# A fused two-layer adapter block on one core: Wb and the first two tiles of W1 multiplied by pairs of k, and five smaller reorderings

## The chip, the core and the metric

The kernel runs on one core of a Trainium2 chip. Such a core has TensorE (PE, with PEld for its weight loads), VectorE (DVE), ScalarE (ACT), GpSimd (POOL) and SyncE (SP, which here only issues transfers), each with an instruction stream of its own, and 16 DMA engines. The streams meet only at semaphores. The metric is device time in microseconds (us), less is better.

## The reference, cut to what matters

Two layers, each a conditional projection followed by a routed low-rank (LoRA) stage, for x of 2048 tokens by 1024 features:

```python
x = x + L0_ffn(L0_cond(x))          # top-2 gated adapters, then top-1 gated low-rank stage
x = x + L1_ffn(L1_cond(x))

# L1_cond: per batch b an adapter slot
out = einsum('bti,oi->bto', x, W) + b + lora_out * SCALING   # A, B of slot adapter_mapping[b]
# L1_ffn: top-2 of 8 experts of rank 16
base = xf @ W_base.T + b_base
logits = xf @ W_router.T
lora = einsum('td,erd->ter', xf, A) ... * SCALING
```

`W` of L1_cond is called W1 below, and `W_router`, `A` and `W_base` of L1_ffn side by side are called Wb: 8 + 128 + 1024 = 1160 columns.

## The kernel before, in words

**What is precomputed.** Nothing lies between L1_cond and L1_ffn but linear maps, so the kernel first multiplies them into one matrix, M = W1 x Wb (plus the identity for the residual), and the main part, one slot for each of the 8 batches, then multiplies x by M. This text is about the part that makes M and about what stands between, the first 166 us or so.

**How M is made.** W1 is cut into eight tiles s = 0 to 7 of 128 rows (rows in the order of `M_ROWS`). Wb lies in SBUF in eight slices k of 128 rows, and by columns in three chunks c = 0, 1, 2 of 240, 460 and 460 (`CHUNKS`). Each product is done as three matmuls of fp32r (`three`, L1332 to L1336): each operand is split into a part hi, which ACT copies, and a part lo, which DVE computes as raw minus hi (`lo`, L850). So a part that lands from DRAM goes DMA, ACT, DVE, PE, in that order. `m_chunk(par, c)` is 8 slices of k times three, 24 matmuls, into a PSUM bank of tile par = s mod 2.

**The opening.** Both tiles of W1 and all of Wb are split as they land. `WF_PARTS` (L274) cuts the tiles of W1, `F_PARTS` (L282) cuts Wb; SP issues the loads in the order of L346 to L355, ACT and DVE split in the same order (L670, L1144), PE takes chunk 0 of both tiles first, then chunk 1 of both by pairs of k, then chunk 2 of tile 0 and of tile 1 (L1377 to L1397). The four engines go by hand-written order alone.

**After it, by the same matmul stream.** (1) The gathered adapters of the slots (`bs_raw`, eight transfers whose addresses SP reads from `ids`) are multiplied by Wb, L1399 to L1407; `keep_fe` stores the result to DRAM (`fe_hi_dram`, `fe_lo_dram`, L377). (2) R0 x B0 (`d0w`), then R0 x W0 for eight tiles of W0, whose homes in SBUF (`W0_HOME`) are used again and again: tile 1 lies where the first tile of W1 was, tile 4 where B0 was. (3) Tiles s = 2 to 7 of W1, and between them the first slot's small products.

**`fold_rows(s)`** (L1120) finishes tile s: `add_ident` on DVE adds the identity in PSUM, ACT splits tile s + 2 of W1 (`w1_split`) into the place that tile s leaves, ACT copies the finished columns, DVE computes their lo parts (`Mdir`, `G`). Before it uses PSUM bank par again, PE waits for `m_lo`, and for `w1_lo` before it uses the split tile (L1447, L1465).

**`b_times(k)`** (L1091) accumulates b x Wb in `b_acc` on DVE: for hi and lo of slice k and the three chunks one instruction each, six in all. There are 8 such k. PE reads `b_acc` in `bias_part` only after tile 7's chunk 0 (L1470).

Of the kernel before, what the change touches and what calls it, by code (L numbers as in the profile page):

```python
# [24 lines left out]
def adaln_ffn(nc, xT, lang_ids, slot_ids, W0, R0, A0, B0, Bw, W1, b1, lora_As, lora_Bs, F0, F1, F2, b_base, B1, out):  # L25
# [11 lines left out]
    with ctx:  # L37
# [122 lines left out]
        wf_in, wf_hi, wf_lo = [sem(f"wf_in{i}") for i in range(5)], sem("wf_hi"), sem("wf_lo")  # L160
# [113 lines left out]
        WF_PARTS = [(0, 0, 2), (0, 2, 4), (1, 0, 4), (0, 4, 8), (1, 4, 8)]  # L274
# [7 lines left out]
        F_PARTS = [(0, 0, 2), (0, 2, 4), (0, 4, K), *((c, k, k + 2) for c in (1, 2) for k in range(0, K, 2))]  # L282
# [45 lines left out]
        def _(sp):  # L328
# [54 lines left out]
            sp.wait_ge(fe_stored, 32)  # L383
# [45 lines left out]
            sp.wait_ge(fe_stored, 64)  # L429
# [63 lines left out]
        def _(gp):  # L493
# [63 lines left out]
        def _(act):  # L557
# [132 lines left out]
            hi_half(bs_in, 16 * NB, k_first(bs_hi_t), by_batch(bs_raw), bs_hi)  # L690
# [38 lines left out]
            for s in range(2, LAST):  # L729
# [49 lines left out]
            act.wait_ge(fe_stored, 64)  # L779
# [69 lines left out]
        def _(dve):  # L849
# [481 lines left out]
        def _(pe):  # L1331
# [373 lines left out]
```

## Time and profile before

| what | value |
|---|---|
| median of 3 runs | 466.93 us (466.07 to 467.23) |
| the profiled execution | 465.49 us, span of its instructions 463.6 us |
| PE busy | 446.5 us, 96% of the span |
| DVE, ACT, POOL busy | 307.6, 154.8, 68.6 us |
| read from DRAM, written | 27.07 MB, 9.59 MB |

The profile is one execution. Its busy times say which engine carries the span; its waits and its timeline say when that engine stood still and for whom. A matmul's end is modelled and overlaps the next one's start, so the distance of two starts is what one costs.

### The profile page before, as it was taken

Reading aid. Unit: us, or ns where it says so; the run is one execution under the profiler, and the core shown is the slowest. Engines: PE = TensorE matmul, PEld = TensorE weight load, DVE = VectorE, ACT = ScalarE, POOL = GpSimd, SP = SyncE. Lnnn points to the kernel's source line nnn. Section 1 sums busy time; section 2 is a strip of 40 time slices with the busy share of each in tenths; the row PEclk is TensorE's granted clock in tenths of the full one; section 3 lists DMA queues with packets and bytes.
Section 4 is the critical chain, followed back from the end, with each engine's and each line's share of the span. In section 5 each row is a group of like instructions: output and inputs, shape, how many; then the busy total and the mean of one; then the engine's idle time right before and its main releaser. Section 6 shows DMA issues by size and latency. Waiting matters only on the chain.

```text
span 463.6 us, 7831 instructions
## 1 busy us (share of the span) xinstructions
PE 446.5 (96%) x2758; PEld 414.8 (89%) x2758; DVE 307.6 (66%) x916; ACT 154.8 (33%) x325; POOL 68.6 (15%) x61
## 2 busy tenths in 40 slices
PE   4999989999969999999999999999999999999997
PEld 4988989999968898889899999999999999999986
DVE  4856675656996788578467648738747755864852
ACT  5754363202122463234233224224323423321310
POOL 1100000000002411402402222120140230220110
PEclk9999999999998999999999999999999999999999
DMA  8973651101110101104102201211210310300202
GB/s 270 386 216 134 207 216 45 47 0 47 53 39 6 50 23 49 47 17 145 47 11 104 79 17 62 98 46 62 98 45 17 139 54 1 111 7 1 107 2 90
DMA packets 16287, 37.08 MB, mean 80 GB/s; under 512 B 2551, under 2 KB 7929, under 8 KB 16254
## 3 DMA queue, kind: packets, MB, share of 16 engines
q1 hardware_dynamic: 16158, 36.66, 23.1%
q8 instruction: 18, 0.29, 0.3%
q14 instruction: 15, 0.12, 0.1%
q0 software_dynamic: 96, 0.00, 0.0%
HBM read 27.07 MB, written 9.59 MB: 79 GB/s over the span
## 4 chain that ended last, share of the span: by engine, by line
PE 72%; DVE 14%; SPq 6%; DMA 3%; issue 2%; ACT 2%; DVEq 0%; ACTq 0%
PE banks L1334 22%; PE banks L1336 22%; PE banks L1335 22%; SPq L330 5%; DVE b_acc L1097 3%; DVE G L852 3%; PE banks L1422 2%; PE banks L1567 2%; DMA ws_lo_raw<-in_W_dram 2%; DMA b0lo_raw<-in_W_dram 1%; DVE ws_lo L852 1%; PE banks L1349 1%; SPq L362 1%; DVE x_raw L998 1%; DVE left L852 1%
## 5 line engine op out<-in xcount | busy, mean ns | idle before, releaser
L1334 PE MATMUL banks<-G,left 128*128 128x460 f32 x224 | 88.0, 393 | 0.0
L1335 PE MATMUL banks<-G,left 128*128 128x460 f32 x224 | 82.9, 370 | 0.0
L1336 PE MATMUL banks<-G,left 128*128 128x460 f32 x224 | 82.9, 370 | 0.0
L1334 PE MATMUL banks<-WbThi,ws_hi 128*128 128x460 f32 (+1 forms) x192 | 68.4, 356 | 9.8 <-DVE WbTlo L852 5.5
L509 POOL TENSOR_TENSOR xTlo<-x_raw,xThi 128x512 fp32r<-128x512 f32 x28 | 37.9, 1373 | 209.7 <-DVE hg L910 107.4
L1336 PE MATMUL banks<-WbThi,ws_lo 128*128 128x460 f32 (+1 forms) x192 | 67.0, 349 | 0.0
L1335 PE MATMUL banks<-WbTlo,ws_hi 128*128 128x460 f32 (+1 forms) x192 | 66.9, 348 | 0.0
L561 ACT ACTIVATE left<-x_raw 128x512 fp32r<-128x512 f32 x64 | 38.7, 627 | 59.9 <-DVE x_raw L998 29.3
L1334 PEld LDWEIGHTS banks<-WbThi,ws_hi 128*128 128x128 f32 x192 | 38.0, 198 | 13.1 <-issue 6.2
L1334 PEld LDWEIGHTS banks<-G,left 128*128 128x128 f32 x224 | 42.5, 190 | 4.5 <-DVE wzTlo L852 0.3
L1336 PEld LDWEIGHTS banks<-G,left 128*128 128x128 f32 x224 | 42.0, 188 | 4.7
L1335 PEld LDWEIGHTS banks<-G,left 128*128 128x128 f32 x224 | 42.3, 189 | 2.6
L998 DVE TENSOR_TENSOR x_raw<-banks,x_raw 128x512 f32<-128x512 f32 x32 | 22.0, 690 | 30.5 <-PE banks L1336 29.6
L1335 PEld LDWEIGHTS banks<-WbTlo,ws_hi 128*128 128x128 f32 x192 | 38.1, 198 | 2.9
L1336 PEld LDWEIGHTS banks<-WbThi,ws_lo 128*128 128x128 f32 x192 | 38.0, 198 | 2.7
L1029 DVE TENSOR_TENSOR ybuf<-banks,ybuf 128x460 f32<-128x460 f32 x48 | 29.6, 629 | 11.4 <-PE banks L1336 10.5
L1334 PE MATMUL banks<-Mdir,left 128*128 128x256 f32 x128 | 36.5, 285 | 0.2 <-DVE left L852 0.2
L1335 PE MATMUL banks<-Mdir,left 128*128 128x256 f32 x128 | 35.9, 281 | 0.0
L1336 PE MATMUL banks<-Mdir,left 128*128 128x256 f32 x128 | 35.9, 281 | 0.0
L509 POOL TENSOR_TENSOR left<-x_raw,left 128x512 fp32r<-128x512 f32 x16 | 20.7, 1311 | 99.4 <-DVE hg L910 74.5
L852 DVE SCALAR_TENSOR_TENSOR left<-x_raw,left 128x512 fp32r<-128x512 f32 x48 | 32.2, 685 | 2.8 <-ACT left L561 1.9
L1336 PE MATMUL banks<-C0hi,xTlo 128*128 128x272 f32 x112 | 32.3, 288 | 0.0
(208 smaller groups left out, 964.1 us busy)
## 6 DMA issues: line engine op xcount, KB each, us to landing
x_raw<-in_xT_dram SPq DMA_DIRECT2D x16, 512.0 KB, 3.7
out_dram<-ybuf SPq DMA_DIRECT2D x14, 512.0 KB, 2.7
WbTlo_raw<-in_F_dram SPq DMA_DIRECT2D x8, 460.0 KB, 8.3
x_raw<-in_W_dram SPq DMA_DIRECT2D x6, 512.0 KB, 3.7
ws_lo_raw<-in_W_dram SPq DMA_DIRECT2D x3, 512.0 KB, 5.1
w0s_lo_raw<-in_W_dram SPq DMA_DIRECT2D x2, 512.0 KB, 9.5
Fbuf<-fe_hi_dram SPq DMA_DIRECT2D x16, 64.0 KB
ws_lo_raw<-in_W_dram SPq DMA_DIRECT2D x3, 256.0 KB, 5.0
```

Source lines behind the costliest of these rows:

```text
L330: return sp.dma_start(dst, src).then_inc(s, 16)
L509: return gp.tensor_tensor(out_, a, b, ALU.subtract)
L561: act.activation(dst, src, ACT.Copy).then_inc(ready, 1)
L852: return dve.scalar_tensor_tensor(out=out_, in0=src, scalar=scale, in1=hi.bitcast(F32), op0=ALU.mult, op1=ALU.subtract)
L998: dve.tensor_tensor(raw_quarter(raw, g), by_half(bank), raw_quarter(raw, g), ALU.add).then_inc(x1_sum, 1)
L1029: return dve.tensor_tensor(ybuf[tile][:, y0:y0 + n], bank, base, ALU.add).then_inc(ready, 1)
L1097: dve.scalar_tensor_tensor(out=b_acc[:, c0:c0 + w], in0=Wb_of[c][n][:, k, :].bitcast(F32), scalar=bcol[:, k:k + 1], in1=b_acc[:, c0:c0 + w ...
L1334: pe.matmul(out_, l[0], r[0], start=start, stop=False, **kw)
L1335: pe.matmul(out_, l[0], r[1], start=False, stop=False, **kw)
L1336: return pe.matmul(out_, l[1], r[0], start=False, stop=stop, **kw)
L1422: ins = pe.matmul(banks[:, C0_BANKS[k // 2] + k % 2, 0:2 * RC], w, R0T[:, j, :], start=j == 0 and n == 0, stop=j == K - 1 and n == 1)
L1567: pe.matmul(y, hsT[half][:, :], Fbuf[:, s], start=False, stop=True, skip_group_check=True)\
```

## The change

It has six parts. (a) The opening: the two tiles of W1 and Wb land and are split by pairs of k over all columns, and PE multiplies both tiles by each part as it comes (`first_two`). W1's two tiles now land in six parts, Wb still in eleven. (b) `b_times` takes a range of halves (hi or lo of one k) in place of a k, and the 16 halves are dealt out to other places of DVE's stream. (c) GpSimd issues the two `ids` loads at once. (d) The split of `bs_raw` stands before `fold_rows(0)` on ACT and DVE. (e) The product of the adapters is stored chunk by chunk, six stores in place of two, and W0's tile 3 is loaded between them. (f) In `fold_rows` on ACT, `w1_split` no longer waits for the identity's addition.

```diff
-        WF_PARTS = [(0, 0, 2), (0, 2, 4), (1, 0, 4), (0, 4, 8), (1, 4, 8)]
+        WF_PARTS = [(0, 0, 2), (1, 0, 2), (0, 2, 4), (1, 2, 4), (0, 4, K), (1, 4, K)]
-        F_PARTS = [(0, 0, 2), (0, 2, 4), (0, 4, K), *((c, k, k + 2) for c in (1, 2) for k in range(0, K, 2))]
+        F_PARTS = [(0, 0, 2), (1, 0, 2), (2, 0, 2), (0, 2, 4), (1, 2, 4), (2, 2, 4),
+                   (0, 4, K), (1, 4, 6), (2, 4, 6), (1, 6, K), (2, 6, K)]
...
+            def store_fe(c):
+                s = slice(CHUNKS[c][0], CHUNKS[c][0] + CHUNKS[c][1])
+                sp.wait_ge(fe_hi, c + 1)
+                sp.wait_ge(fe_lo, c + 1)
+                sp.dma_start(fe_hi_dram[0:P, s], fe_keep[0][:, s].bitcast(F32)).then_inc(fe_stored, 16)
+                sp.dma_start(fe_lo_dram[0:P, s], fe_keep[1][:, s].bitcast(F32)).then_inc(fe_stored, 16)
+
+            store_fe(0)
+            store_fe(1)
             sp.wait_ge(fe_done, 3)
             load_w0(3)
-            sp.wait_ge(fe_hi, 3)
-            sp.wait_ge(fe_lo, 3)
-            sp.dma_start(fe_hi_dram[0:P, :], fe_keep[0][:, :].bitcast(F32)).then_inc(fe_stored, 16)
-            sp.dma_start(fe_lo_dram[0:P, :], fe_keep[1][:, :].bitcast(F32)).then_inc(fe_stored, 16)
+            store_fe(2)
             sp.wait_ge(d0w_done, 1)
             load_w0(4)
             sp.wait_ge(c0_used, 1)
             load_w0(5)
-            sp.wait_ge(fe_stored, 32)
+            sp.wait_ge(fe_stored, 96)
             load_w0(6)
...
-            gp.wait_ge(wf_hi, 5)
             gp.dma_start(ids[0:1, 0:NB], ...
             gp.dma_start(ids[0:1, NB:2 * NB], ...
+            gp.wait_ge(wf_hi, 6)
...
             hi_half(a0_in, 16, a0_part(C0hi), a0_part(C0raw), a0_hi)
+            hi_half(bs_in, 16 * NB, k_first(bs_hi_t), by_batch(bs_raw), bs_hi)
             act.wait_ge(m_ident, 1)
...
-            hi_half(bs_in, 16 * NB, k_first(bs_hi_t), by_batch(bs_raw), bs_hi)
             act.wait_ge(bs_lo, 1)
...
-                act.wait_ge(m_ident, s + 1)
                 act.wait_ge(m_done, m_count(s, 2))
                 w1_split(s + 2)
+                act.wait_ge(m_ident, s + 1)
                 keep(direct(0, row), m_psum(par, 0), m_hi)
...
             gates0(0, 0)
-            hgT_part(0)
             dve.wait_ge(bcol_in, 16)
             dve.wait_ge(bbase_in, 16)
-            b_times(0)
+            b_times(0, 1)
+            hgT_part(0)
+            b_times(1, 4)
             top1(0)
             fold_rows(2)
             whT_part(0, 0)
             gates0(1, 0)
+            b_times(4, 5)
             hgT_part(1)
-            b_times(1)
+            b_times(5, 8)
             top1(1)
             fold_rows(3)
             whT_part(1, 1)
+            b_times(8, 11)
             for g in range(2):
                 x1_add(0, g, x_raw0, X1W_FIRST[g])
-            b_times(2)
             fold_rows(4)
             for g in range(2, 4):
                 x1_add(0, g, x_raw0, X1W_FIRST[g])
-            for k in range(3, 6):
-                b_times(k)
+            b_times(11, 2 * K)
             fold_rows(5)
-            for k in range(6, K):
-                b_times(k)
...
+            def first_two(c, k0, k1, split):
+                for par in range(2):
+                    pe.wait_ge(f_lo, split)
+                    if c == 0:
+                        pe.wait_ge(wf_lo, min(2 * (k0 // 2), 4) + par + 1)
+                    m_steps(par, c, k0, k1)
+
+            first_two(0, 0, 2, 1)
+            first_two(1, 0, 2, 2)
+            first_two(2, 0, 2, 3)
...
```

**DVE between tile 4 and tile 5.** The row on `ident` is `add_ident` of `fold_rows`, `ws_lo` is the split of the next tile of W1, the rows of `b_acc` are halves of `b_times` (a half is one row of 240 columns and one `x2` of 460). Before:

```order
L1108 TENSOR_TENSOR banks<-banks,ident 128x128
L852 SCALAR_TENSOR_TENSOR ws_lo<-x_raw,ws_hi 128x1024
L852 SCALAR_TENSOR_TENSOR Mdir<-banks,Mdir 128x240
L998 TENSOR_TENSOR x_raw<-banks,x_raw 128x2x2x128 x2
L1097 SCALAR_TENSOR_TENSOR b_acc<-WbThi,bcol,b_acc 128x240
L1097 SCALAR_TENSOR_TENSOR b_acc<-WbThi,bcol,b_acc 128x460 x2
...
L1108 TENSOR_TENSOR banks<-banks,ident 128x128
L852 SCALAR_TENSOR_TENSOR ws_lo<-x_raw,ws_hi 128x1024
L852 SCALAR_TENSOR_TENSOR Mdir<-banks,Mdir 128x240
L1097 SCALAR_TENSOR_TENSOR b_acc<-WbThi,bcol,b_acc 128x240
```

Now:

```order
L1125 TENSOR_TENSOR banks<-banks,ident 128x128
L869 SCALAR_TENSOR_TENSOR ws_lo<-x_raw,ws_hi 128x1024
L869 SCALAR_TENSOR_TENSOR Mdir<-banks,Mdir 128x240
L1015 TENSOR_TENSOR x_raw<-banks,x_raw 128x2x2x128 x2
L1114 SCALAR_TENSOR_TENSOR b_acc<-WbTlo,bcol,b_acc 128x240
L1114 SCALAR_TENSOR_TENSOR b_acc<-WbTlo,bcol,b_acc 128x460 x2
...
L1125 TENSOR_TENSOR banks<-banks,ident 128x128
L869 SCALAR_TENSOR_TENSOR ws_lo<-x_raw,ws_hi 128x1024
L869 SCALAR_TENSOR_TENSOR Mdir<-banks,Mdir 128x240 x3
```

Six halves stood between the two tiles and four after the second; now five stand between and none after it.

**SP around the stores of the adapters' product.** `bs_lo_t_raw` is tile 3 of W0, `b0lo_raw` tile 4, `w0s_lo_raw` tile 5, `xT_second_lo_raw` tile 6. Before:

```order
L330 DMA bs_lo_t_raw<-in_W_dram 128x1024 [waits fe_done]
L377 DMA fe_hi_dram<-fe_keep_hi 128x1160 [waits fe_lo,fe_hi]
L378 DMA fe_lo_dram<-fe_keep_lo 128x1160
L330 DMA b0lo_raw<-in_W_dram 128x1024 [waits d0w_done]
L330 DMA w0s_lo_raw<-in_W_dram 128x1024 [waits c0_used]
L330 DMA xT_second_lo_raw<-in_W_dram 128x1024 [waits fe_stored]
```

Now:

```order
L383 DMA fe_hi_dram<-fe_keep_hi 128x240 [waits fe_lo,fe_hi]
L384 DMA fe_lo_dram<-fe_keep_lo 128x240
L383 DMA fe_hi_dram<-fe_keep_hi 128x460 [waits fe_lo,fe_hi]
L384 DMA fe_lo_dram<-fe_keep_lo 128x460
L331 DMA bs_lo_t_raw<-in_W_dram 128x1024 [waits fe_done]
L383 DMA fe_hi_dram<-fe_keep_hi 128x460 [waits fe_lo,fe_hi]
L384 DMA fe_lo_dram<-fe_keep_lo 128x460
L331 DMA b0lo_raw<-in_W_dram 128x1024 [waits d0w_done]
L331 DMA w0s_lo_raw<-in_W_dram 128x1024 [waits c0_used]
```

Tile 3's load moved from before all stores to behind the stores of chunks 0 and 1; chunk 0 is stored while later chunks are still being made.

## Rows read from the trace of the kernel before

**Rows 1.** The page, busy time: engine, us, share of span, instructions.

```profile
PE 446.5 (96%) x2758; PEld 414.8 (89%) x2758; DVE 307.6 (66%) x916; ACT 154.8 (33%) x325; POOL 68.6 (15%) x61
```

**Rows 2.** Waits of PE: who waited for whom, us in total, times, longest.

```profile
PE banks L1334 <- DVE WbTlo L852: 5.5, 1, 5.5
PE banks L1334 <- DVE Mdir L852: 3.8, 1, 3.8
PE banks L1422 <- DVE b0lo L852: 1.4, 1, 1.4
PE banks L1334 <- DVE bs_lo_t L852: 1.2, 1, 1.2
```

**Rows 3.** A stretch: bounds, length, busy of each engine, clock, DMA share, GB/s.

```profile
138.10:141.40 3.30, 3.30 (x16) 3.25 (x15) 3.30 (x8) 0.37 (x1) 0.00 (x0) 0.50 0.31 112
```

**Rows 4.** Timeline of PE, tile 6's chunk 0 ends, tile 7's chunk 0 begins.

```profile
132.66 0.28 PE L1336 MATMUL banks<-WbThi,ws_lo 128*128 128x240 f32 x1
136.68 0.35 PE L1334 MATMUL banks<-WbThi,ws_hi 128*128 128x240 f32 x1 [3.75 <-DVE Mdir L852]
```

**Rows 5.** Timeline of DVE, from the small products to tile 5: start, us, instruction.

```profile
115.42 1.41 DVE L998 TENSOR_TENSOR x_raw<-banks,x_raw 128x512 f32<-128x512 f32 x2 [4.03 <-PE banks L1336]
...
122.81 1.28 DVE L998 TENSOR_TENSOR x_raw<-banks,x_raw 128x512 f32<-128x512 f32 x2
124.00 1.67 DVE L1097 SCALAR_TENSOR_TENSOR b_acc<-WbThi,bcol,b_acc 128x240 f32<-128x240 f32 x3
...
133.58 0.29 DVE L1108 TENSOR_TENSOR banks<-banks,ident 128x128 f32<-128x128 f32 x1
134.99 1.23 DVE L852 SCALAR_TENSOR_TENSOR ws_lo<-x_raw,ws_hi 128x1024 fp32r<-128x1024 f32 x1 [1.12 <-ACT ws_hi L561]
136.13 0.40 DVE L852 SCALAR_TENSOR_TENSOR Mdir<-banks,Mdir 128x240 fp32r<-128x240 f32 x1
```

**Rows 6.** Timeline of ACT at tile 5.

```profile
133.90 1.06 ACT L561 ACTIVATE ws_hi<-x_raw 128x1024 fp32r<-128x1024 f32 x1 [11.44 <-DVE banks L1108]
```

**Rows 7.** Timeline of DVE, its idle times at the small transposes.

```profile
80.52 0.29 DVE L852 SCALAR_TENSOR_TENSOR hgTlo<-banks,hgThi 128x128 fp32r<-128x128 f32 x1 [3.10 <-ACT hgThi L561]
...
96.81 0.29 DVE L852 SCALAR_TENSOR_TENSOR hgTlo<-banks,hgThi 128x128 fp32r<-128x128 f32 x1 [2.36 <-ACT hgThi L561]
```

**Rows 8.** Stretches of the opening and of the adapters' product, columns as in Rows 3.

```profile
5.50:11.50 6.00, 5.48 (x24) 5.23 (x24) 3.46 (x6) 3.64 (x6) 0.40 (x1) 1.00 0.97 364
...
35.90:38.70 2.80, 2.80 (x25) 2.80 (x26) 1.23 (x1) 1.08 (x2) 0.00 (x0) 1.00 0.93 369
```

**Rows 9.** Timeline of ACT: a part of W1, the adapters, tiles 1, 3 and 4 of W0.

```profile
6.60 0.42 ACT L561 ACTIVATE ws_hi<-ws_lo_raw 128x256 fp32r<-128x256 f32 x1 [1.29 <-DMA ws_lo_raw<-in_W_dram]
...
38.66 1.06 ACT L561 ACTIVATE ws_hi<-ws_lo_raw 128x1024 fp32r<-128x1024 f32 x1 [1.72 <-DMA ws_lo_raw<-in_W_dram]
...
52.29 1.06 ACT L561 ACTIVATE bs_hi_t<-bs_lo_t_raw 128x1024 fp32r<-128x1024 f32 x1 [0.47 <-DMA bs_lo_t_raw<-in_W_dram]
...
58.63 1.06 ACT L561 ACTIVATE b0hi<-b0lo_raw 128x1024 fp32r<-128x1024 f32 x1 [1.69 <-DMA b0lo_raw<-in_W_dram]
```

**Rows 10.** Timeline of SP: when the load of tile 3, the stores and tile 4 were issued.

```profile
48.90 0.33 SPq L330 DMA_DIRECT2D bs_lo_t_raw<-in_W_dram  x1
51.61 0.35 SPq L377 DMA_DIRECT2D fe_hi_dram<-fe_keep_hi  x1
```

**Rows 11.** Timeline of DVE, the lo parts of chunks 1 and 2 of the adapters' product.

```profile
50.35 1.18 DVE L852 SCALAR_TENSOR_TENSOR fe_keep_lo<-banks,fe_keep_hi 128x460 fp32r<-128x460 f32 x2
```

**Rows 12.** Stretch in which the two stores ran, columns as in Rows 3.

```profile
52.40:56.20 3.80, 3.80 (x33) 3.80 (x32) 1.40 (x2) 1.35 (x2) 0.00 (x0) 1.00 1.01 346
49.90:52.00 2.10, 2.10 (x20) 2.10 (x20) 1.74 (x7) 0.28 (x1) 0.00 (x0) 1.00 0.71 254
```

**Rows 13.** Timeline of PE, tiles 3 and 4 of W0 begin.

```profile
57.40 0.29 PE L1422 MATMUL banks<-R0T,bs_hi_t 128*128 128x272 f32 x1
...
61.00 0.39 PE L1422 MATMUL banks<-R0T,b0hi 128*128 128x272 f32 x1 [1.44 <-DVE b0lo L852]
```

More of the change, by code:

```diff
@@ L159, in adaln_ffn @@
         w0_in, w0_hi, w0_lo = [sem(f"w0_in{i}") for i in range(K)], sem("w0_hi"), sem("w0_lo")
-        wf_in, wf_hi, wf_lo = [sem(f"wf_in{i}") for i in range(5)], sem("wf_hi"), sem("wf_lo")
+        wf_in, wf_hi, wf_lo = [sem(f"wf_in{i}") for i in range(6)], sem("wf_hi"), sem("wf_lo")
         b0_in, b0_hi, b0_lo = sem("b0_in"), sem("b0_hi"), sem("b0_lo")
@@ L347, in _ @@
             load_f(0)
+            load_wf(1)
             load_f(1)
-            load_wf(1)
+            load_f(2)
             load_wf(2)
+            load_f(3)
             load_wf(3)
-            load_f(2)
+            load_f(4)
+            load_f(5)
             load_wf(4)
-            for i in range(3, 11):
+            load_f(6)
+            load_wf(5)
+            for i in range(7, 11):
                 load_f(i)
@@ L428, in _ @@
             sp.dma_start(fe_lo_dram[P:P + 1, :], b_acc[32:33, :]).then_inc(fe_stored, 16)
-            sp.wait_ge(fe_stored, 64)
+            sp.wait_ge(fe_stored, 128)
             sp.wait_ge(memsets_done, 2)
@@ L671, in _ @@
             f_split(0)
+            wf_split(1)
             f_split(1)
-            wf_split(1)
+            f_split(2)
             wf_split(2)
+            f_split(3)
             wf_split(3)
-            f_split(2)
+            f_split(4)
+            f_split(5)
             wf_split(4)
-            for i in range(3, 11):
+            f_split(6)
+            wf_split(5)
+            for i in range(7, 11):
                 f_split(i)
@@ L778, in _ @@
             act.wait_ge(g2_lo, 7)
-            act.wait_ge(fe_stored, 64)
+            act.wait_ge(fe_stored, 128)
             a_part(0, 0, 1)
@@ L1088, in keep_fe, with b_times @@
                 lo(fe_keep[1][:, c0:c0 + n], m_psum(0, c), fe_keep[0][:, c0:c0 + n], 2.0).then_inc(fe_lo, 1)
-            def b_times(k):
-                for n in range(2):
+            def b_times(first, last):
+                for nth in range(first, last):
+                    k, n = nth // 2, nth % 2
                     for c, (c0, w) in enumerate(CHUNKS):
-                        nth = 2 * k + n
                         dve.wait_ge(acc_step, 3 * nth + c - 1 if nth else 1)
@@ L1145, in _ @@
             f_split(0)
+            wf_split(1)
             f_split(1)
-            wf_split(1)
+            f_split(2)
             wf_split(2)
+            f_split(3)
             wf_split(3)
-            f_split(2)
+            f_split(4)
+            f_split(5)
             wf_split(4)
-            for i in range(3, 11):
+            f_split(6)
+            wf_split(5)
+            for i in range(7, 11):
                 f_split(i)
@@ L1156, in _ @@
             lo_in(a0_hi, 1, a0_part(C0lo), a0_part(C0raw), a0_part(C0hi), a0_lo)
+            lo_in(bs_hi, 1, k_first(bs_lo_t), by_batch(bs_raw), k_first(bs_hi_t), bs_lo)
             dve.wait_ge(ident_ready, 1)
             fold_rows(0)
-            lo_in(bs_hi, 1, k_first(bs_lo_t), by_batch(bs_raw), k_first(bs_hi_t), bs_lo)
             w0_split(0)
@@ L1375, in m_chunk @@
                 m_steps(par, c, 0, K)
-            pe.wait_ge(wf_lo, 1)
-            pe.wait_ge(f_lo, 1)
-            m_steps(0, 0, 0, 2)
-            pe.wait_ge(f_lo, 2)
-            pe.wait_ge(wf_lo, 2)
-            m_steps(0, 0, 2, 4)
-            pe.wait_ge(wf_lo, 3)
-            m_steps(1, 0, 0, 4)
-            pe.wait_ge(wf_lo, 4)
-            pe.wait_ge(f_lo, 3)
-            m_steps(0, 0, 4, K)
-            pe.wait_ge(wf_lo, 5)
-            m_steps(1, 0, 4, K)
-            for k in range(0, K, 2):
-                pe.wait_ge(f_lo, 4 + k // 2)
-                for par in range(2):
-                    m_steps(par, 1, k, k + 2)
-            for k in range(0, K, 2):
-                pe.wait_ge(f_lo, 8 + k // 2)
-                m_steps(0, 2, k, k + 2)
-            m_chunk(1, 2)
+            def first_two(c, k0, k1, split):
+                for par in range(2):
+                    pe.wait_ge(f_lo, split)
[5 more added lines that the diff above has]
+            first_two(2, 0, 2, 3)
+            first_two(0, 2, 4, 4)
+            first_two(1, 2, 4, 5)
+            first_two(2, 2, 4, 6)
+            first_two(0, 4, 6, 7)
+            first_two(1, 4, 6, 8)
+            first_two(2, 4, 6, 9)
+            first_two(0, 6, K, 7)
+            first_two(1, 6, K, 10)
+            first_two(2, 6, K, 11)
             pe.wait_ge(bs_lo, 1)
```

2 lines of the change are left out of this document (1 added, 1 removed).

## The prediction

> **What bounds the kernel now.** I read the page's busy times first: PE is busy for 96% of the span and DVE for 66% [rows 1]. So only two things can shorten the run, less time in which PE stands still and less time in which it works at its lower clock; work taken off another engine counts only through these. Next the waits of PE [rows 2]. Four matter: 5.5 us at the start until the first parts are split, 1.2 for the lo part of the adapters (`bs_lo_t`), 1.4 for the lo part of W0's tile 4 (`b0lo`), and 3.8 for `Mdir`, a lo part that DVE makes in `fold_rows(5)`. The timeline of PE puts the last at 132.9 to 136.7, between tile 6's chunk 0 and tile 7's [rows 4]. Behind it the clock matters: from 138.1 to 141.4 the granted clock is 0.50, that is 1.2 GHz instead of 2.4 [rows 3]. PE had stood still for 3.75 us shortly before. In those 3.3 us PE did 1.65 us of work of full clock. The stall so costs 3.75 + 1.65 = 5.4 us in all.
>
> **Part (b), the halves of b_times.** Why is `Mdir` late? DVE runs the 18 instructions of `b_times` for k = 3 to 5 in one piece from 124.0 to 133.6: six halves, 9.6 us, 1.6 each [rows 5] (the first of six such rows). PE finished tile 5 at about 130.1, since tile 6's chunk 0, 24 matmuls at 2.80/25 = 0.112 us [rows 8], ends at 132.9 [rows 4]. Only at 133.58 comes `add_ident`, then ACT's split of W1's tile 7 at 133.90 for 1.06 [rows 6], then DVE's at 134.99, and `Mdir` at 136.13 to 136.53 [rows 5]. In the new order five halves stand here, and three before the two `x1_add` that begin at 115.42. Those three, 4.8 us, fit nearly into the 4.03 us of idle time ahead of 115.42 [rows 5], since part (f) also lets `fold_rows(3)` end about 1.1 us earlier (the row of ACT's wait, 1.12 us before `ws_lo`, is what goes). Two other halves go into the idle 3.10 and 2.36 us ahead of the two `hgTlo` [rows 7], 1.6 into each. With `fold_rows(4)` no longer behind six instructions, the second pair of `x1_add` becomes bound by PE's products, at most as late as before, so it ends by 124.0 [rows 5] and I expect nearer 121; five halves then end at 129 (132.0 at worst).
>
> From there the new chain is: tile 5 done on PE at 130.1; ACT's split no longer waits for `add_ident`, so it runs 130.15 to 131.2 and both begin together; DVE's split to 132.4, `Mdir` to 132.8 (the same durations 1.06, 1.23 less overlap, 0.40). PE wants it at 132.9. So the wait is 0 to 0.2 us where it was 3.75, and with no stall I see nothing that lowers the clock. I take 5.3 us of gain. Should the halves end only at 132.0, `Mdir` comes at 134.6, PE waits 1.8 us, and the gain is 3.6 if the clock keeps up. The four halves behind tile 5 are gone too, and nobody waited for them. What is late next is PE itself: after this point every chain (bias, right factors) starts from its products and moves with it.
>
> **Part (a), the opening.** The first 240-column part of each matrix lands as before, so PE starts at 5.5 again. The matmuls are the same 48 of 240 columns and 96 of 460. At full clock they are 48 x 0.112 + 96 x 0.215 = 26.0 us (0.215 is 0.112 x 460/240). Before, PE began at 5.5 and ended at 34.7 (35.9 less the wait of 1.2 [rows 2, 8]); the difference of 3.2 us is 0.5 of idle and half-rate work: 5.48/24 = 0.228 us a matmul up to 11.5 against 0.112 later [rows 8], so 1.2 GHz. In the new order PE needs a part of 0.47 MB of chunk 1 after only 12 matmuls, at 5.5 + 12 x 0.228 = 8.2. The part of W1 that landed at 6.6 [rows 9] had 0.75 MB before and with it; chunk 1's first part has 0.98 MB, so at 364 GB/s [rows 8] it lands at 7.2, and with ACT's and DVE's splits (2.1 us for 920 columns, by the 1.06 and 1.23 for 1024) it is ready at 9.4. PE idles 1.2 us instead of 0.5, and if the clock rises up to 3 us later, loses up to 1.5 more. Afterwards a pair of k is 1.42 MB, 3.9 us of transfer, for 6.5 us of work: PE is ahead of nothing. The opening ends between 34.5 and 37.
>
> What is that worth? Nothing up to 37.3, because the two waits behind it absorb it: PE waited 1.2 us for the adapters and 1.4 for tile 4 of W0. The latter does not come from PE. It goes back over the stores to DVE's `fe_keep_lo` at 50.35 [rows 11], and DVE had been working without a pause since tile 1 of W0 landed, at 38.66 [rows 9], behind the loads of x, which are issued before it. The new order frees tile 1's home later, at about 33.2 (6 matmuls of 460 columns, 1.3 us, before the end). A load like tile 3's took 3.4 us from issue to ACT, 48.90 to 52.29 [rows 9, 10], which gives 36.6 and leaves the landing at 38.66 to what is ahead of it in the queue. So this landing stays, in both directions: an earlier end gains nothing either. Parts (c) and (d) can save at most the 1.2 of [rows 2], and the same wait for tile 4 takes it back. Their value is zero, and without that cover it would be up to 1.2.
>
> **Part (e), the stores.** Before: tile 3's load issued at 48.90, split from 52.29; stores issued from 51.61; tile 4 split from 58.63 [rows 9, 10]. Now SP waits first for chunk 1's lo part, 51.0 [rows 11], issues 0.47 MB of stores, tile 3 (0.52 MB), again 0.47 MB and tile 4. At 346 GB/s [rows 12] tile 3 comes 2.1 + 1.4 = 3.5 us later, at 55.8, and is ready for PE 2.4 later at 58.2; PE wants it at 57.40 [rows 13]. A stall of 0.8 us, inside the 1.44 of tile 4. Tile 4: before 1.71 MB from 51.61, now 1.99 MB from 51.0: +0.8 - 0.6 = +0.2 us, and ACT's and DVE's small steps for tile 3's sums may add as much. I take 0.2 us of loss. Bounds: if landings become quicker the wait of 1.4 can vanish, -1.4. If the smaller stores run at the 254 GB/s that a single load reached [rows 12], 0.94 MB take 1.0 us longer, +1.2; both stores also waiting out a latency like tile 3's gives about +3.5.
> The Trainium skill, page "DMA: Bandwidth & Descriptors", section "Bandwidth", says that transfers should be batched to 1 MiB, and puts 1 MB at 341 GB/s and 64 KB at 138, which speaks against cutting two stores into six; by an estimate between these figures, 200 GB/s for 0.24 MB, part (e) would cost 2.2 us instead of 0.2. The loads of 0.13 to 0.47 MB in the opening moved at 364 GB/s one behind another [rows 8], so I stay with the row.
>
> **The sum.** The profiled execution is 465.49 us: 465.49 - 5.3 + 0.2 = 460.4. The median of the runs, 466.93, lies 1.44 above it, and it is what will be compared: **461.8 us**.
>
> **The rivals.**
> A, the stores bite: tile 3 and tile 4 of W0 stand in a full queue behind them. For it: tile 4's wait is already the limit there. Against: chunk 0's stores leave before DVE reaches 50.35 and are out of the way. 1.2 to 3.5 us of loss: 463.0 to 465.3, say 464.0. Chance 0.15.
> B, tile 4's wait vanishes, with tile 1 landing earlier: 460.4. Nothing but the queue's jitter speaks for it. 0.10.
> C, `Mdir` stays late by up to 1.8 us because the five halves start late: 463.6 at the worst. Against it stands the slack of 1 us or more worked out above. 0.07.
> D, slower: PE is starved in the opening and stays at 1.2 GHz. The new order makes PE wait for each part in turn. All of it at the lower rate would be 48 x 0.228 + 96 x 0.437 = 52.9 us, the end at 58.4, 21.1 us past the cover of 37.3: 482.9. It decides at an end of 37.3 + 5.3 = 42.6, that is with low clock until about 28. For it: idle time in front of low clock is seen in this trace [rows 3, 4]. Against: 3.9 us of transfer for 6.5 of work at full rate, and more at half. A mild case, 43.5, gives 467.8. Chance 0.03.
> The Trainium skill, page "TensorE: Matmul & The Clock Gate", section "HAM oscillation — how this bites in real kernels", advises to do all k tiles of one output before the next wait for DMA, since short bursts between waits let the clock fall each time; the change goes the other way, and by that rule D would be the outcome, 482.9. The fall at 138.1 agrees with the rule; that the opening has such waits the transfer rate does not bear out.
> That the change does not do what it says (no halves out of the way) the new order excludes.
>
> **How the numbers follow.** Main case 0.65, A 0.15, B 0.10, C 0.07, D 0.03. Range: from B's end with 0.5 for the spread of medians, 459.9, to A's middle, 464.2. A measurement here tells 0.3%, 1.4 us, from no change. All but D, and A's and C's worst ends with extra noise (0.03), are faster by more: 0.93; within 0.3%: 0.04; slower: 0.03.
>
> **What would show it.** In PE's waits `Mdir` should be gone or under 0.3 us, with no stretch of low clock near 138. The waits for `b0lo` and for tile 3 together should be 1 to 3 us, PE starting tile 4 within 0.5 us of 61.0. The opening should end between 34.5 and 37, with a first idle time near 8.2. I am wrong if a stall of over 1 us stands between tile 5 and tile 7, if tile 4 starts after 62.5, or if the opening ends after 37.3.

## The result, and the profile after

The changed kernel took 461.11 us (median of 4 runs, 460.7 to 461.34) against 466.86 for the kernel before on the same chip (466.07 to 467.23): ratio 0.9885, 95% interval 0.9868 to 0.9902. It is faster by 5.4 us at that ratio; 461.8 was predicted, in a range of 459.9 to 464.2. The profiled executions are 465.49 and 461.34 us, their spans 463.6 and 459.5.

PE's busy time and its waits on the page of the changed kernel (the waits: us in total, times, longest), to be held against [rows 1, 2]:

```profile
PE 445.1 (97%) x2758; PEld 413.1 (90%) x2758; DVE 307.7 (67%) x917; ACT 154.4 (34%) x326; POOL 68.6 (15%) x61
```

```profile
PE banks L1355 <- DVE WbTlo L869: 5.8, 2, 5.5
PE banks L1441 <- DVE bs_lo_t L869: 1.4, 1, 1.4
PE banks L1355 <- DVE Mdir L869: 1.2, 1, 1.2
PE banks L1370 <- DVE wz L927: 0.8, 1, 0.8
PE banks L1441 <- DVE b0lo L869: 0.8, 1, 0.8
```

The 3.8 us for `Mdir` at tile 7 are gone. The 1.2 us under the same name belong to another place: the adapters' chunk 0 waits for `fold_rows(0)`, which now stands behind DVE's 2.20 us for the adapters. The 1.4 under `bs_lo_t` are not the adapters either, but tile 3 of W0, whose home has the same name. A group of waits goes by names, so each has to be looked up in the timeline:

```profile
35.55 0.35 PE L1355 MATMUL banks<-WbThi,bs_hi_t 128*128 128x240 f32 x1 [1.18 <-DVE Mdir L869]
...
58.64 0.39 PE L1441 MATMUL banks<-R0T,bs_hi_t 128*128 128x272 f32 x1 [1.44 <-DVE bs_lo_t L869]
61.66 0.40 PE L1441 MATMUL banks<-R0T,b0hi 128*128 128x272 f32 x1 [0.76 <-DVE b0lo L869]
```

```profile
32.09 2.20 DVE L869 SCALAR_TENSOR_TENSOR bs_lo_t<-bs_raw,bs_hi_t 128x1024 fp32r<-128x1024 f32 x1 [3.18 <-ACT bs_hi_t L573]
```

Tile 5 of M, on DVE and then on ACT, to be held against [rows 5, 6]:

```profile
121.59 1.68 DVE L1114 SCALAR_TENSOR_TENSOR b_acc<-WbTlo,bcol,b_acc 128x240 f32<-128x240 f32 x3
...
131.01 0.30 DVE L1125 TENSOR_TENSOR banks<-banks,ident 128x128 f32<-128x128 f32 x1 [1.36 <-PE banks L1357]
132.10 1.23 DVE L869 SCALAR_TENSOR_TENSOR ws_lo<-x_raw,ws_hi 128x1024 fp32r<-128x1024 f32 x1 [0.80 <-ACT ws_hi L573]
133.25 0.40 DVE L869 SCALAR_TENSOR_TENSOR Mdir<-banks,Mdir 128x240 fp32r<-128x240 f32 x1
```

```profile
131.01 1.06 ACT L573 ACTIVATE ws_hi<-x_raw 128x1024 fp32r<-128x1024 f32 x1 [11.94 <-PE banks L1357]
```

DVE now reaches `add_ident` 1.36 us before PE has the product, and ACT and DVE start together at 131.01. PE begins tile 7's chunk 0 at 133.79, right behind tile 6's, and the stretch that had run at 0.50 [rows 3] has its full clock (bounds, length, busy time of each engine, granted clock, DMA share, GB/s):

```profile
138.10:141.40 3.30, 3.30 (x18) 2.98 (x17) 0.78 (x1) 0.27 (x2) 2.25 (x2) 1.00 0.00 0
```

Up to the first matmul of W1's tile 2 the changed kernel is later, not earlier: 69.80 against 69.13 us. So in these two executions the parts in front of it cost 0.7 us together, and all of the gain stands behind it, near 138. There 5.4 us went (the stall of 3.75 and 1.7 of low clock), and the span is shorter by 4.1: besides the 0.7, another 0.6 is lost in small amounts between tile 2 and the end.

### The profile page after: what moved, and what is told of

Its sections match the earlier page's. It is cut to its first block, busy times and chain, and to the rows that moved or that the text cites. A ratio compares the mean times of both kernels' runs of the same rounds, so it can differ in the third digit from the quotient of the medians.

```text
span 459.5 us, 7845 instructions
## 1 busy us (share of the span) xinstructions
PE 445.1 (97%) x2758; PEld 413.1 (90%) x2758; DVE 307.7 (67%) x917; ACT 154.4 (34%) x326; POOL 68.6 (15%) x61
## 4 chain that ended last, share of the span: by engine, by line
PE 81%; DVE 11%; DMA 3%; ACT 2%; issue 2%; SPq 0%; DVEq 0%; ACTq 0%
PE banks L1355 25%; PE banks L1357 25%; PE banks L1356 25%; DVE G L869 3%; PE banks L1441 2%; PE banks L1586 2%; DMA ws_lo_raw<-in_W_dram 1%; PE banks L1370 1%; DMA bs_lo_t_raw<-in_W_dram 1%; DMA WbTlo_raw<-in_F_dram 1%; DVE left L869 1%; DVE G_raw L1129 1%; DVE ws_lo L869 1%; PE banks L1495 0%; DVE x_raw L1042 0%
## 5 line engine op out<-in xcount | busy, mean ns | idle before, releaser
L573 ACT ACTIVATE left<-x_raw 128x512 fp32r<-128x512 f32 x64 | 38.7, 627 | 59.9 <-DVE x_raw L1015 29.3
L1357 PEld LDWEIGHTS banks<-WbThi,ws_lo 128*128 128x128 f32 x192 | 37.0, 193 | 2.8
```

The costliest lines, as they stand in the source:

```text
L573: act.activation(dst, src, ACT.Copy).then_inc(ready, 1)
L1357: return pe.matmul(out_, l[1], r[0], start=False, stop=stop, **kw)
```

## The experiments

The runs of before that each ratio is against were taken on the same chip. "Span" is that of the profiled execution.

| kernel | median us | ratio (interval) | span |
|---|---|---|---|
| halves only: (b) | 460.66 | 0.9898 (0.9860 to 0.9936) | 458.6 |
| split first only: (f) | 461.80 | 0.9910 (0.9875 to 0.9945) | 459.8 |
| (b), (f) | 459.84 | 0.9870 (0.9846 to 0.9894) | 457.7 |
| (b), (f), (c), (d) | 460.22 | 0.9872 (0.9839 to 0.9905) | 457.6 |
| (c), (d) only | 466.60 | 1.0013 (0.9991 to 1.0035) | 462.1 |
| (a), (b), (f) | 466.37 | 0.9990 (0.9970 to 1.0009) | 465.7 |
| changed, old stores | 460.67 | 0.9893 (0.9862 to 0.9925) | 459.0 |
| changed, old opening | 460.64 | 0.9897 (0.9863 to 0.9930) | 458.1 |
| changed, once more | 461.61 | 0.9902 (0.9876 to 0.9928) | 460.9 |
| changed, stores last | 460.44 | 0.9878 (0.9854 to 0.9902) | 459.0 |
| the same with the old opening | 460.21 | 0.9860 (0.9840 to 0.9880) | 457.6 |
| changed, opening begun late | 461.07 | 0.9892 (0.9867 to 0.9917) | 460.1 |

### The halves and the split, each alone and together

The halves alone: `b_times` takes a range of halves and DVE's stream has the order of the changed kernel.

> The kernel before with part (b) alone, the halves of b_times dealt out; fold_rows on ACT still waits for the identity first. My theory (the stall of PE for Mdir of tile 5 and the clock that falls behind it are the gain): tile 5 is done on PE at 130.1, add_ident to 130.5, ACT's split to 131.6, DVE's to 132.8, Mdir to 133.2 or a little later, 133.8. PE wants it at 132.9: a wait of 0.4 to 1.0 us instead of 3.75 and no stretch of low clock near 138. Gain 4.4 to 5.0 us against before. Rival 1 (part (f) makes most of the gain): under 3 us. Rival 2 (the gain comes from the opening or the stores): 0.

Measured 460.66, and PE's wait at tile 7 fell from 3.75 to 0.46:

```profile
133.07 0.35 PE L1333 MATMUL banks<-WbThi,ws_hi 128*128 128x240 f32 x1 [0.46 <-DVE Mdir L852]
```

The split alone:

```diff
-                act.wait_ge(m_ident, s + 1)
                 act.wait_ge(m_done, m_count(s, 2))
                 w1_split(s + 2)
+                act.wait_ge(m_ident, s + 1)
```

> The kernel before with part (f) alone, w1_split on ACT ahead of the wait for the identity. My theory: ACT splits tile 7 of W1 while DVE is still in its six halves, so behind add_ident (133.9) DVE splits at once, and Mdir comes 1.1 us earlier, at 135.4 instead of 136.5. PE waits 2.6 us instead of 3.75; the clock still falls unless 2.6 us are too short for that. Gain 1.1 us, or 2.8 if the clock does not fall. Rival (part (f) makes most of the gain): 4 us or more.

Measured 461.80, a gain of 4.2 us by the ratio where 1.1 or 2.8 was expected. PE, then DVE and the stretch behind the wait:

```profile
134.02 0.35 PE L1334 MATMUL banks<-WbThi,ws_hi 128*128 128x240 f32 x1 [1.30 <-DVE Mdir L852]
```

```profile
119.72 0.29 DVE L1108 TENSOR_TENSOR banks<-banks,ident 128x128 f32<-128x128 f32 x1
119.92 1.22 DVE L852 SCALAR_TENSOR_TENSOR ws_lo<-x_raw,ws_hi 128x1024 fp32r<-128x1024 f32 x1
...
122.56 1.68 DVE L1097 SCALAR_TENSOR_TENSOR b_acc<-WbThi,bcol,b_acc 128x240 f32<-128x240 f32 x3
...
132.14 0.29 DVE L1108 TENSOR_TENSOR banks<-banks,ident 128x128 f32<-128x128 f32 x1
132.34 1.22 DVE L852 SCALAR_TENSOR_TENSOR ws_lo<-x_raw,ws_hi 128x1024 fp32r<-128x1024 f32 x1
```

```profile
134.10:140.00 5.90, 5.90 (x40) 5.55 (x41) 5.90 (x12) 0.37 (x1) 0.00 (x0) 1.00 0.27 89
```

Two things were missed. DVE's idle time for ACT's split is saved twice, at tile 4 (the six halves begin at 122.56, not at 124.00 [rows 5]) and at tile 5 (`ws_lo` directly behind `add_ident`). And what is left of the stall, 1.30 us, lowered no clock. With both parts together:

> The kernel before with parts (b) and (f) together and nothing else: b_times by halves dealt out, and ACT's w1_split no longer behind the identity's addition. Each alone gave 4.7 us and 4.2 us (by their ratios to the kernel before of the same chip). Theory (substitutes: both remove the same stall of 3.75 us and the same stretch of low clock of 1.65, and there are only 5.4 us to be had): 5.0 to 5.6 us of gain, a ratio of 0.988 to 0.9895, no wait for Mdir of over 0.2 us at tile 7, no clock fall. Rival (the two add up, since each also moves other things): 8 us or more of gain, ratio under 0.984. Rival 2 (nothing beyond the halves alone): ratio 0.990 and a wait of 0.4 to 0.5 us for Mdir.

Measured 459.84, ratio 0.987: 6.1 us by the ratio, a little above the 5.0 to 5.6 expected, and far from the 8.9 that the two singles would add up to. No wait for `Mdir` stands at tile 7. (b) and (f) are substitutes, and each alone has two thirds or more of the gain. These two parts are already as fast as anything else that ran. (In this execution PE also waited 1.60 us in the opening, at 12.01, and no low clock followed.)

### The stores

The changed kernel with the two whole stores of before, behind tile 3's load:

> The changed kernel with part (e) undone: two whole stores behind tile 3's load, as before. My theory from the trace of the changed kernel: tile 4 of W0 begins there at 61.66, before at 61.00, since tile 3 (begun at 58.64) and tile 4 came late behind the stores. With the old stores tile 3 waits for nothing and tile 4 begins at 60.9 to 61.0: 0.7 us faster than the changed kernel, 0.9 at most. If the small stores pay by leaving earlier (the rival), it is slower than the changed kernel.

Measured 460.67. There is no wait for tile 3, 1.87 us for tile 4, which begins at 61.26, and W1's tile 2 begins at 69.39 against 69.80. The clock stays at 1.00 behind this wait, the longest of its kind in these traces (PE's row, then the stretch):

```profile
61.26 0.39 PE L1435 MATMUL banks<-R0T,b0hi 128*128 128x272 f32 x1 [1.87 <-DVE b0lo L863]
```

```profile
61.30:64.60 3.30, 3.30 (x26) 3.30 (x27) 3.30 (x4) 2.70 (x5) 0.00 (x0) 1.00 0.12 30
```

The gain over the changed kernel is 0.4 us in the trace, less than the 0.7 to 0.9 expected; the medians don't resolve it. A second pair that differs by (e) alone, with the old opening, shows 0.7 us: W1's tile 2 begins at 68.11 without (e), in the kernel with (b), (c), (d) and (f), and at 68.78 with it.

Why tile 4 is late in the changed kernel ACT's rows show. It splits tile 4 (`b0hi`) with no idle time ahead of it, right behind a small step for tile 3's sum (`C0hi`) that waited for DVE, and that chain goes back to the landing of tile 3 (`bs_hi_t`), for which ACT waited 4.81 us:

```profile
56.27 1.06 ACT L573 ACTIVATE bs_hi_t<-bs_lo_t_raw 128x1024 fp32r<-128x1024 f32 x1 [4.81 <-DMA bs_lo_t_raw<-in_W_dram]
...
58.97 0.43 ACT L573 ACTIVATE C0hi<-C0lo_raw 128x272 fp32r<-128x272 f32 x1 [1.36 <-DVE C0lo_raw L902]
59.30 1.04 ACT L573 ACTIVATE b0hi<-b0lo_raw 128x1024 fp32r<-128x1024 f32 x1
```

Then the changed kernel itself, once more:

> The changed kernel itself, so that the others of this series are compared with it on one chip. 0.9885 of before within 0.002. Its profile should again show no stall for Mdir over 0.2 us at tile 7 and tile 4 of W0 beginning at 61 to 62 after two waits.

The ratio is 0.9902, and no stall for `Mdir` stands at tile 7. Its profiled execution shows a larger stall before tile 3 of W0, and low clock behind it; tile 4 begins at 62.52, where 61 to 62 and two waits were expected, behind this one wait:

```profile
59.49 0.40 PE L1441 MATMUL banks<-R0T,bs_hi_t 128*128 128x272 f32 x1 [1.78 <-DVE bs_lo_t L869]
```

```profile
60.90:64.20 3.30, 3.22 (x14) 2.90 (x14) 2.97 (x3) 3.30 (x5) 0.00 (x0) 0.50 0.54 212
```

So in this execution the stall cost 1.7 us more than its length. Of ten executions of the changed kernel, two have a mean granted clock of 0.995 or 0.996 and took 462.8 and 463.3; the other eight have 0.999 or 1.000 and took 460.6 to 461.7. That part (e) brings the falls is not shown. They come without it too: the kernel with the old stores has a mean clock of 0.996 in one of four executions, and the one with (b), (c), (d) and (f) has 0.995 or 0.996 in three of six (460.8 to 462.5 us, against 459.2 to 459.6 at 1.000). Next, chunks 1 and 2 are stored only behind W0's tile 5:

```diff
             store_fe(0)
-            store_fe(1)
             sp.wait_ge(fe_done, 3)
             load_w0(3)
-            store_fe(2)
             sp.wait_ge(d0w_done, 1)
             load_w0(4)
             sp.wait_ge(c0_used, 1)
             load_w0(5)
-            sp.wait_ge(fe_stored, 96)
-            load_w0(6)
+            store_fe(1)
+            store_fe(2)
             sp.wait_ge(c0_used, 3)
+            load_w0(6)
+            sp.wait_ge(fe_stored, 96)
             load_w0(7)
```

(Tiles 6 and 7 exchange their homes.)

> The changed kernel with the stores of chunks 1 and 2 issued behind the loads of W0's tiles 3, 4 and 5, and the homes of tiles 6 and 7 exchanged so that only tile 7 waits for the stores. My theory: tiles 3 and 4 waited only because their loads stood behind 0.94 MB of stores. Tile 3 is issued at 48.6 and ready by 54.5, tile 4 issued at 51.2 and ready by 57.5, tile 6 issued at 57.3 and ready near 63, so PE runs from 57.2 without a wait and ends the eight tiles at 67.2 instead of 69.8: 2.0 to 2.6 us faster than the changed kernel (458.6 to 459.2 where that one has 461.1). Rival (something else is late next): the waits move to tiles 5 or 6 and under 1 us is gained.

Measured 460.44 against 461.61 for the changed kernel beside it. The waits for tiles 3 and 4 are gone, and tile 6 has one instead:

```profile
65.18 0.39 PE L1441 MATMUL banks<-R0T,ws_hi 128*128 128x272 f32 x1 [1.47 <-DVE ws_lo L869]
```

It came out nearer to the rival's side. In these orders the stores' bytes stood in front of some tile each time: tile 6's load, issued behind them at 57.39, reached ACT 5.4 us later (62.81), where tile 3's, ahead of them, took 3.6. Two waits of 2.20 us together became one of 1.47, and W1's tile 2 begins at 69.48 instead of 69.80. All six executions had a clock of 0.999 or 1.000. Falls of the clock are not what most of the 1.2 us is: the eight executions of the changed kernel without one have a median of 461.2 (the four beside it 461.5), still 0.8 above. The rest of it these runs do not explain.

### The opening

The changed kernel with part (a) undone:

> The changed kernel with part (a) undone: opening, landing order and parts as before. My theory: the opening's end is covered by the waits for tiles 3 and 4 of W0, which come from DVE's chain behind tile 1's landing at 38.6; tile 4 begins at 61.7 as in the changed kernel and the time is the same within 0.3 us, although the two openings end at different times. Rival (the new opening is part of the gain): 0.5 us or more slower than the changed kernel.

Measured 460.64, the same within the noise. The cover was not quite as expected: tile 4 of W0 begins at 60.66, not at 61.7, behind waits of 1.29 us for tile 3 and 0.75 for tile 4, so the old opening is 1.0 us ahead there in the trace. To test the cover, the changed kernel with its first matmul held until chunk 1's first part is split, `first_two(0, 0, 2, 2)` in place of `(0, 0, 2, 1)`:

> The changed kernel with PE's first matmul held until the first part of chunk 1 is split too, so that it starts near 8.7 instead of 5.45 us; nothing else is changed. The opening then ends 2 to 3 us later, at 36.4 to 37.4 instead of 34.4. My theory (the waits behind the opening cover it, up to about 36.5, where tile 1 of W0 would land later): the time is 0 to 0.9 us longer than the changed kernel's. Rival (no cover, each microsecond of the opening counts): 2 to 3 us longer.

Measured 461.07, beside 461.61 for the changed kernel. PE:

```profile
9.11 0.57 PE L1355 MATMUL banks<-WbThi,ws_hi 128*128 128x240 f32 x1 [9.11 <-DVE WbTlo L869]
...
37.35 0.28 PE L1355 MATMUL banks<-WbThi,bs_hi_t 128*128 128x240 f32 x1
...
59.54 0.39 PE L1441 MATMUL banks<-R0T,bs_hi_t 128*128 128x272 f32 x1 [0.63 <-DVE bs_lo_t L869]
62.56 0.39 PE L1441 MATMUL banks<-R0T,b0hi 128*128 128x272 f32 x1 [0.75 <-DVE b0lo L869]
```

PE starts 3.7 us late, and the adapters begin 1.8 later (37.35 against 35.55). By tile 4 of W0 0.9 of it is left, and the span is 0.6 us longer. The cover is real, if not whole.

Then (c) and (d) alone, on the kernel before:

> The kernel before with parts (c) and (d) alone, ids issued at once and the adapters split ahead of fold_rows(0). My theory: PE's wait for the adapters becomes one of 0.4 us or more for Mdir of fold_rows(0), and the wait for tile 4 of W0 grows by what was saved: the time is that of before within 0.3 us. The stall at tile 7 is still there, so the profile also shows a second time whether the clock falls behind it and for how long. Rival (the adapters' earlier split is worth its 1.2 us): 1 us faster.

Measured 466.60, no gain in the median. But the trace does not show the theory's mechanism: the adapters begin at 35.00 instead of 35.90, the wait for tile 4 did not grow but fell from 1.44 to 0.81, and tile 4 begins 1.5 us earlier:

```profile
59.46 0.39 PE L1422 MATMUL banks<-R0T,b0hi 128*128 128x272 f32 x1 [0.81 <-DVE b0lo L852]
```

This execution (463.97) is the fastest of ten. Four of the ten have a mean clock of 0.989 or less, against one of 17 of the kernel before beside it; the three at 0.996 have a median of 464.8 against 465.7 at that clock. So a gain of about 1 us, the rival, is not excluded. The stall at tile 7 stands as before, with its low clock (PE's row, then the stretch):

```profile
135.19 0.35 PE L1334 MATMUL banks<-WbThi,ws_hi 128*128 128x240 f32 x1 [3.74 <-DVE Mdir L852]
```

```profile
136.40:139.70 3.30, 3.30 (x17) 3.30 (x16) 3.30 (x7) 0.04 (x1) 0.00 (x0) 0.50 0.39 120
```

And (a) without (c) and (d), on top of (b) and (f):

> Parts (a), (b) and (f) on the kernel before: the halves, the split and the new opening, nothing else. Beside it stand (b) and (f) without the opening: 459.8 us, ratio 0.987, span 457.7. The prediction took the opening at zero. But in the traces so far W0's tile 1 reached ACT at 38.6 to 39.6 us with the new opening and at 37.5 to 38.7 with the old, and the span was 1.3 to 1.4 us longer in both pairs that differ by it. Theory (the new opening costs about 1 us, through the later end of the chunks and the later landing of tile 1): span 458.7 to 459.2, 0.7 to 1.5 us slower than (b) and (f) alone, ratio 0.989 to 0.991. Rival (zero, as predicted, the spans were chance): ratio 0.986 to 0.988, span 457.4 to 458.2.

Neither theory: 466.37, that is 6 us slower than (b) and (f) alone, the whole gain lost. POOL, ACT, then PE, then three stretches behind:

```profile
16.90 0.67 POOL L508 DMA_DIRECT2D ids<-in_lang_ids_dram  x1 [15.20 <-ACT ws_hi L567]
```

```profile
36.58 0.59 ACT L674 ACTIVATE G<-G_raw 128x460 fp32r<-128x460 f32 x1 [0.70 <-DVE G_raw L1123]
37.07 2.02 ACT L567 ACTIVATE bs_hi_t<-bs_raw 128x1024 fp32r<-128x1024 f32 x1
```

```profile
41.17 0.57 PE L1349 MATMUL banks<-WbThi,bs_hi_t 128*128 128x240 f32 x1 [4.63 <-DVE bs_lo_t L863]
```

```profile
39.70:41.10 1.40, 0.00 (x0) 0.00 (x0) 1.40 (x1) 0.00 (x0) 0.00 (x0) 0.50 0.97 363
41.20:46.40 5.20, 5.20 (x25) 5.20 (x26) 3.13 (x5) 3.19 (x5) 0.00 (x0) 0.52 0.27 110
46.60:50.00 3.40, 3.40 (x18) 3.08 (x17) 3.40 (x7) 1.72 (x4) 0.00 (x0) 1.00 0.00 0
```

With pairs of k over all columns both tiles finish together at the end of the opening. `fold_rows(0)`, which ACT had done by 31.5 before, now lasts until 37.07, and in the old order the adapters' split stands behind it. The row of `bs_hi_t` shows no idle time ahead of it: ACT, not the transfer, set it (the last of the adapters' loads was issued at 31.7 and none took over 2.7 us to land). PE waits 4.63 us, and its next 24 matmuls take 5.18 us instead of 2.79, since the clock has fallen. That is 4.63 + 2.4 = 7.0, against 1.18 for the adapters in the kernel with (b) and (f) alone. The opening itself ended 1.5 us later than there (36.54 against 35.06), and W1's tile 2 begins 7.6 us later (75.92 against 68.35). (`ids`, behind the wait for ACT's sixth part, is issued at 16.90 instead of 11.10 and makes the adapters' loads issue at 23.61, not at 18.46; with (c) they were issued at 19.21. This alone would not have been seen, as ACT came later still. Which of (c) and (d) is the one that counts was not tried apart.) Against the kernel that differs by (c) and (d) alone, the changed kernel with the old stores, the loss is 4.5 us by the ratios (0.9990 and 0.9893) and 5.7 by the medians.

(c) and (d) beside (b) and (f), with neither (a) nor (e):

> Parts (b), (c), (d) and (f) on the kernel before, that is the changed kernel without the new opening and without the new stores. Prediction's theory (the end of the adapters' wait of 1.2 us is taken back at tile 4 of W0, so parts (c) and (d) are worth nothing): as (b) and (f) alone, ratio 0.986 to 0.988, wait for b0lo about 1.2 us longer than there, tile 4 of W0 begun at 60.2 to 61. Rival (the pause at tile 4 does not grow, since W0's tile 1 lands earlier too, as in the run of (c) and (d) alone, where tile 4 began at 59.46): up to 1.2 us faster, ratio 0.984 to 0.9855, tile 4 begun before 59.8.

Measured 460.22: no gain over (b) and (f). PE waits for `b0lo` 0.79 us instead of 0.32, and tile 4 of W0 begins at 59.98 instead of 60.22; the adapters began 0.6 us earlier (35.64 against 36.24), and all but 0.24 of that is taken back. Last, old opening and late stores together:

> The changed kernel with the opening as before (part (a) undone) and with the stores of chunks 1 and 2 issued behind the loads of W0's tiles 3, 4 and 5 (tiles 6 and 7 exchange their homes), so the two single steps of which one cost nothing and the other gained 0.9 to 1.2 us. Theory: the opening is worth zero in either order, so this is as fast as the stores' step alone, 0.9 to 1.2 us below the changed kernel, ratio to before 0.9870 to 0.9885, tile 6 of W0 waited for 1 to 1.5 us and no clock fall. Rival (the new opening was worth something once the waits for tiles 3 and 4 that covered it are gone): 1 us or more slower than that, ratio 0.990 or more.

Measured 460.21, ratio 0.986, a little below the 0.9870 to 0.9885 expected, with 1.25 us of wait for tile 6 of W0 and no fall of the clock.

Three pairs of these kernels differ by the opening alone. Begin of W1's tile 2 with the old opening and with the new: 68.11 and 69.39 (old stores), 68.44 and 69.48 (stores last), 68.78 and 69.80 (stores of the changed kernel). Each time the new one is 1.0 to 1.3 us later, and the span 1.4 longer. By the ratios the difference is 1.0, 0.8 and between -0.6 and 0.2 us, with intervals of over 1 us each: the traces of six single executions say about 1 us, the medians do not resolve it. In the same three pairs W0's tile 1 reaches ACT later by 0.80, 1.05 and 1.10 us, so most of the difference is there already at that point. Its load is issued at 33.2 to 34.5 with the new opening and at 30.3 to 30.8 with the old.

A rival for part of it is the clock in the opening. The distance of two matmuls shows when PE goes over to its full rate (0.21 us for 240 columns before, 0.11 behind it); the profile's clock column says 1.00 for the slow part too, in [rows 8] as well, and cannot be used there. With the old opening that is at 9.5 to 13.8 us in eight executions, with the new at 11.8 to 15.6 in six (14.9 in the one begun late). It fits the second and third pair (10.4 and 14.4, 9.9 and 11.8) and not the first, where the old opening is the later one (13.8 and 13.2). Whether the new opening makes the full rate come later these runs do not tell.

## Why the prediction was right, point by point

**What bounds.** Right. The stall of 3.75 us and the low clock behind it were the gain: every kernel with (b) or (f) gained 4 to 6.5 us, but for the one that lost as much in its opening, and the one without them gained nothing in the median.

**Part (b) with (f), 5.3 us.** Right in mechanism and nearly in size. The product of tile 5 was expected at 130.1 and came at 131.0, as all before it is 0.7 later; the split and `Mdir` followed in the predicted steps (132.10 and 133.25, against 131.2 and 132.4), and PE waited no more. The prediction took (f) as a help for (b), and alone it gives 4.2 us.

**Part (a), zero.** This step failed, though the sum did not show it. Its numbers for PE were nearly right: the opening ended at 34.4 (34.5 to 37 was given), with the first idle time at 8.4 (8.2), 0.32 us long (1.2; 0.76 to 1.29 in four other executions with this opening). Its cover was incomplete. The prediction held the end of the opening against 37.3 and saw no more; it did not ask what ACT does when tile 0 and tile 1 finish together. Without (c) and (d) the adapters' split would have stood behind `fold_rows(0)`, 6 us; with it, DVE's 2.20 us for the adapters stand ahead of `fold_rows(0)`, and PE waited 1.18 for `Mdir` at 35.55. And the landing of W0's tile 1, which was to "stay", did so against the one trace that the prediction had (38.60 and 38.66), but not over all: it reached ACT between 37.5 and 38.7 in eight executions with the old opening, and between 38.6 and 39.3 in four with the new (39.6 where it was begun late). Its home was free at 33.15, as given (33.2), but the load then took 5.4 us to reach ACT and not the 3.4 taken from tile 3's. Whether the later issue or the rest of the queue sets the landing is not shown.

**Parts (c) and (d), zero.** By the medians right on the kernel before and on (b) and (f) (466.60; and 460.22 beside 459.84), though that tile 4 takes the saving back is seen only in the second, not in the trace of the first. It is wrong beside (a): there they are worth some 5 us (4.5 by the ratios, 5.7 by the medians). The values of parts are not to be added up one by one.

**Part (e), 0.2 us of loss.** The direction was right and the size too small. Tile 3 was given as ready at 58.2 and PE began it at 58.64. Tile 4 was given within 0.5 of 61.0 and began at 61.66, outside that; it was reckoned from its own bytes, and what made it late was the chain behind tile 3's landing, which the prediction had only as a possible addition. The two waits together are 2.2 us (1 to 3 was given). Against the old stores the traces show 0.4 and 0.7 us of loss in two pairs; the falls of the clock by 1.7 us more came with the old stores too. The estimate by the Trainium skill, page "DMA: Bandwidth & Descriptors", section "Bandwidth", was 2.2 us of loss; the 0.4 and 0.7 do not bear it out.

**The offset.** 1.44 us between the profiled execution and the median of three runs was carried over unchanged. Over 52 further runs of the kernel before the median is 466.2, and the profiled 465.49 is only 0.7 below. Their mean granted clock is a part of why such a figure moves: the 21 with 0.995 or 0.996, as in the profiled one, have a median of 465.9, the 31 with 0.993 or less one of 466.6. The rest of the spread is not the clock. The median of all ten runs of the changed kernel is 461.4; so the gain is nearer to 4.8 us than to the 5.4 of the first ratio, and 5.1 was predicted. That the forecast of 461.8 came within 0.7 is partly luck: the profiled execution was forecast at 460.4 and took 461.34, 0.9 too little, and the offset to the median was taken as +1.44 and was -0.2, 1.7 too much; the two errors cancel in part.

**Rivals.** A did not come in the measured sizes, though the stall of 1.78 us with low clock behind it, in one trace of the changed kernel, is a mild form of it. B did not: PE waited 0.76 us for tile 4. C did not. D did not come in the changed kernel: the opening's waits were 5.45 and 0.32 us. Its first 24 matmuls of 460 columns took 6.5 us from 8.69 on, the next 24 took 5.0, so the full rate came at 11.8, where it had come before at 11.9, and stayed. In the other executions with this opening it came at 13.2 to 15.6 and stayed through the opening too; a mild form of D, worth 0.7 to 1.9 us (half of the 1.4 to 3.8 by which it came later than 11.8), is not excluded. The Trainium skill's rule on waits between short bursts (page "TensorE: Matmul & The Clock Gate", section "HAM oscillation — how this bites in real kernels") was not borne out in the opening itself, where the waits behind the first matmul were 0.32 us, and at most 1.29 in the other traces with this order. In the kernel with (a) but without (c) and (d) the low clock did come, in a wait of 4.63 us. That agrees with the rule in so far as a wait of 3 to 5 us stands at the fall; it was one wait for ACT's and DVE's splits behind a long run of matmuls, not one of many between short bursts.

## What to carry to other kernels

Look first for the engine's stall with low clock behind it, and ask which of its two ends is cheaper to move: here one line that lets ACT start early gave most of what dealing out sixteen halves gave. When an order changes so that two results finish together, list what every helping engine has queued behind the first of them, and move it in the same edit. A part that is worth nothing alone may be what keeps another from costing some 5 us, so undo parts in pairs before one is called free.

## What the runs showed of the chip

Stalls of PE of 1.30 us (split alone), 1.44 us (the changed kernel, tile 3 of W0), 1.60 us (opening of (b) and (f)) and 1.87 us (old stores, tile 4 of W0) had no low clock behind them. One of 1.78 us did, as did those of 3.74, 3.75 and 4.63 us. So in this range the length alone does not decide it: 1.78 us had a fall and 1.87 us had none. The low clock set in while or after PE stood, and lasted for at least 3.3 us behind the first three, with PE busy nearly throughout; with the stall of 4.63 it was there from 39.4, in the stall, to 46.2. The stalls of 1.44 and 1.78 us are two executions of the same kernel, so there the price of a stall was its length in one and 1.7 us more in the other. What else decides it these runs do not tell.

In the opening the full rate of PE came between 9.5 and 15.6 us in 14 executions, a spread worth up to 3 us by an estimate (half of the 6.1), more than most of the single steps compared here.
